# Moving the out projection, the residual sum and its statistics one unit later in a fused Mamba and mixture-of-experts kernel

## The chip, the cores and the metric

The kernel runs on one core of a Trainium2 chip. The metric is the time of one execution on the device, in microseconds (us). The engines are named as in the profile: PE is TensorE, DVE is VectorE, ACT is ScalarE, POOL is GpSimd, SP is the engine that issues most DMAs.

## What is computed

The input x has 2 sequences of 2048 tokens with 128 numbers each. The reference, cut down:

```python
def mamba_layer(x):                       # x: layer norm of the input
    u  = ln(x) * n1_g + n1_b
    xin, z = split(u @ in_proj_w.T)       # 256 channels each
    xc = silu(causal_conv4(xin) + conv_b)
    dt, B, C = split(xc @ x_proj_w.T)     # 8, 16, 16
    delta = softplus(dt @ dt_w.T + dt_b)
    # for each of the 16 states n, along the tokens t:
    #   h[n] = exp(delta * A[n]) * h[n] + delta * B[n] * xc ;  y += h[n] * C[n]
    y = (y + xc * D) * silu(z)
    x = x + y @ out_w.T                   # out projection and residual sum
    n = ln(x) * n2_g + n2_b               # the statistics of this norm move
    gate, val = split(n @ ffg_w.T + ffg_b)
    return x + silu(gate) * val @ ffp_w.T + ffp_b

x = x + mamba_layer(layernorm(x))
x = x + top2_of_8_experts(layernorm(x))   # width 344, routed token by token
```

All is in float32.

## The kernel before

The 4096 tokens are cut into 8 chunks of 512, four sub-blocks of 128. A chunk has 16 **units**, one for each state, numbered here 0 to 15 (so that the fourth unit is unit 3). A unit i does this for both halves of the 256 channels:

- GpSimd multiplies `du` with a row of B that a DMA has spread over the partitions: `inflow` (L818), 128x1024. It is written two units ahead, into one of three buffers, so it waits for the product of unit i - 3 relative to its own (`times_c`).
- ScalarE writes `decay` (L941) into two PSUM banks, one unit ahead.
- VectorE does the scan over the tokens (L1077), two instructions of 128x512. One operand lies in PSUM, one in SBUF.
- VectorE multiplies the states with a spread row of C: `product` (L1087), with both operands in SBUF. TensorE adds the product up in PSUM (L1284, "total"). In some units two or four of the four sub-blocks take another way: TensorE turns the states (L1313, "h_turn"), ScalarE scales them into `h_rows` (L906), TensorE adds them (L1288). Then the product has only half its width (128x512), or there is none.

A chunk's work ahead of its units (the first norm, the convolution, delta: the "front" of chunk c + 1, table `FRONT`) and behind them (gate, out projection, second norm, feed-forward layer, third norm, routing: the "back" of chunk c - 1, table `BACK`) is dealt out over the units of chunk c, a row of the table for each unit. The tokens of earlier chunks go through the experts meanwhile: `silu_m` (L1213), `h_cols` (L1218), `y_rows` (L997), and the "add" (L848), an indirect DMA that GpSimd issues. Routed tokens are sent by "scatter" (L842), another indirect DMA of GpSimd, from table `SEND` or, for the last chunks, `SEND_HELD`; neither has anything in unit 4.

A row of `BACK` has three parts: ahead of the unit's scan, behind the scan, and at the unit's end. One list `order` holds all steps; each engine walks through it and issues the instructions of its own steps in that order. The steps within unit i, from the function `plan`:

```python
        fetch("inflow", i + 2)
        ...
            put("total0", i - 1)
        ...
        put_all(back[0], front[0])
        add()
        put("scan", i)
        ...
        put_all(back[1])
        ...
        first_half(m)
        put_all(back[2], front[2])
        ...
        send()
        ...
        put("times_c", i)
```

The steps that the change touches:

- `y_cols0`, `y_cols1` (L951, ScalarE): the gated y, turned, from PSUM to SBUF.
- `out_proj` (L1332, TensorE): 16 matmuls of 128x128 into the PSUM bank `work_side`. It waits for both `y_cols`.
- `x_two` (L1099, VectorE): the residual sum, 128x512, from SBUF and `work_side`. It waits for `out_proj`.
- `stats2` (L1007 and L1010, VectorE): four statistics and four aggregates.
- `rstd2` (L801 and L803, GpSimd): the variance plus epsilon, to the power -1/2. It waits for the aggregates.
- `shift2` (L1013, VectorE): minus mean times `rstd`, 128x4, both operands in SBUF. It waits for `rstd2`; behind it come `n_tok` (L957, ScalarE, written into the tile m_tok) and `n_turn` (L1224, TensorE).

The front has its own steps in these units: `in1a` and `in1b` (L1248, TensorE) at the ends of units 2 and 3, `conv1` and `tanh_c` (L883, L886, ScalarE) in unit 4, and `xc` (L1045, VectorE) behind shift2 in unit 5. The back of the last chunk, `BACK_LAST`, runs behind the units.

Of the kernel before, what the change touches and what calls it, by code (L numbers as in the profile page):

```python
# [32 lines left out]
def sure_tiles(c):  # L33
# [52 lines left out]
BACK = [  # L86
    ((), ("y_gate",), ("y_turn0",)),
    ((), ("y_cols0",), ("y_turn1",)),
    ((), ("y_cols1",), ("out_proj",)),
    ((), ("x_two", "stats2"), ()),  # L90
    (("rstd2",), (), ()),
    ((), ("shift2",), ("n_tok",)),
    (("n_turn",), ("n_t",), ("ff_gate",)),
    (("x_sum",), ("gate_h",), ("ff_val",)),
# [7 lines left out]
    ((), ("count", "place"), ()),  # L102
]
BACK_LAST = [
    *BACK[:3],
    ((), ("x_two", "stats2", "rstd2"), ()),
    *BACK[5:9],
    ((), ("x_four", "stats3", "rstd3"), ()),
# [1352 lines left out]
```

How the kernel before makes its waits and increments, by code:

```python
        def list_steps(e, step_no, key):  # L548
            if step_no == "0":
                at = LIST_OPS * (key - ROUNDS[0])
                k = SPAN_OF[key]
                taken = base[:, 1, k, :] if key == max(ROUNDS[0], SPANS[k][0]) else tiles_done
                e.wait_ge(S["count"], 2 * (key + 1))
                if at:
                    e.wait_ge(S["list"], at)
                else:
                    e.wait_ge(S["bases"], BASES)
                e.tensor_scalar(tiles_f[:], count[:], 1.0 / P, -ROUND_UP, ALU.mult, ALU.add).then_inc(S["list"], 1)
                if key == CHUNKS - 2:
                    e.tensor_scalar(old_end, count[:], 1.0 / P, ROUND_UP, ALU.mult, ALU.add).then_inc(S["ends"], 1)
                    e.wait_ge(S["ends"], 1)
                    e.tensor_scalar(old_end, old_end, WHOLE, -WHOLE, ALU.add, ALU.add).then_inc(S["ends"], 1)
                e.wait_ge(S["list"], at + 1)
                e.tensor_scalar(tiles_f[:], tiles_f[:], WHOLE, -WHOLE, ALU.add, ALU.add).then_inc(S["list"], 1)
                e.wait_ge(S["list"], at + 2)
                e.tensor_tensor(left[:, 0, 4:], tiles_f[:], taken, ALU.subtract).then_inc(S["list"], 1)
                for k in range(3):
                    e.wait_ge(S["list"], at + 3 + k)
# [39 lines left out]
        def last_list(e, step_no, key):  # L609
# [2 lines left out]
            n = TILES[key]  # L612
            if step_no == "0":
                e.wait_ge(S["count"], 2 * (key + 1))
                e.wait_ge(S["list"], at)
```

## Time and profile before

| | |
|---|---|
| median of 3 runs | 851.82 us (850.19 to 853.87) |
| profiled execution | 846.1 us |
| its span | 844.3 us, 12617 instructions |
| busy share of the span | PE 77%, DVE 88%, ACT 60%, POOL 69% |
| mean granted TensorE clock | 0.889 of full speed |

The span is that of the recorded instructions; the profiled execution's own time has about 1.8 us around it. Busy time counts from an instruction's start to its end as recorded, and so holds any time in which it had started and could not go on. Times in the trace are in us from the start of the span.

### The profile page before, as it was taken

How to read it: one execution, taken by the hardware profiler on the slowest of the kernel's cores; microseconds unless marked ns; L12 is line 12 of the kernel's file. 1: busy time of each engine (PE TensorE's matmuls, PEld its weight loads, DVE VectorE, ACT ScalarE, POOL GpSimd, SP SyncE). 2: the span in 40 equal slices, each digit the busy share in tenths (PEclk: the TensorE clock that was granted, in tenths of full speed). 3: DMA queues.
4: the chain of work that ended last, by engine and by line, in shares of the span. 5: the costliest groups of instructions: out<-in, count | busy, mean ns of one | idle time of the engine just before them, and what ended most of it. 6: DMA issues, size and time to landing. Idle time of an engine off the chain costs nothing.

```text
span 844.3 us, 12617 instructions
## 1 busy us (share of the span) xinstructions
PE 649.8 (77%) x3545; PEld 465.3 (55%) x3545; DVE 739.2 (88%) x1145; ACT 506.5 (60%) x1091; POOL 581.2 (69%) x487
## 2 busy tenths in 40 slices
PE   4438688878778877887877876886876789888991
PEld 2124445545355536764566635873554457788990
DVE  1376998989999999999999999999999897686774
ACT  2545795876688577464846577555854775444440
POOL 1094675677977797689958896789846994456451
PEclk9659899989989898997989988897887899999995
DMA  6923233223323336542464336532424621123247
GB/s 175 263 104 103 87 113 113 82 84 97 116 69 107 106 102 182 158 145 99 130 174 140 109 96 203 148 110 94 133 91 128 171 61 33 39 65 83 65 129 231
DMA packets 80248, 99.94 MB, mean 118 GB/s; under 512 B 10215, under 2 KB 48051, under 8 KB 80163
## 3 DMA queue, kind: packets, MB, share of 16 engines
q1 hardware_dynamic: 75859, 90.21, 36.3%
q0 software_dynamic: 4320, 8.92, 3.0%
q8 instruction: 30, 0.49, 0.2%
q14 instruction: 39, 0.32, 0.1%
HBM read 87.56 MB, written 15.35 MB: 122 GB/s over the span
## 4 chain that ended last, share of the span: by engine, by line
DVE 37%; PE 34%; issue 17%; ACT 7%; DMA 2%; POOL 2%; DVEq 1%; SPq 0%; ACTq 0%; POOLq 0%
DVE state L1077 18%; PE work_front L1248 4%; PE y L1288 4%; DVE product L1087 4%; PE up L1399 2%; PE work_front L1254 2%; PE y L1284 2%; PE up L1410 2%; PE gate L1392 2%; DVE stats L1007 2%; ACT decay L941 1%; DVE silu_m L1213 1%; PE gate L1313 1%; DVE arena L1052 1%; PE work_side L1332 1%
## 5 line engine op out<-in xcount | busy, mean ns | idle before, releaser
L818 POOL TENSOR_TENSOR inflow<-du,b_wide 128x1024 f32<-128x1024 f32 x128 | 315.5, 2468 | 145.0 <-DVE product L1087 92.0
L1077 DVE TENSOR_TENSOR_SCAN state<-decay,carry,inflow 128x512 f32<-128x512 f32 x192 | 234.7, 1264 | 6.5 <-ACT decay L941 6.5
L1087 DVE TENSOR_TENSOR product<-state,c_wide 128x1024 f32<-128x1024 f32 (+1 forms) x93 | 139.1, 1495 | 4.4 <-PE y L1284 3.3
L941 ACT ACTIVATE decay<-arena,a_neg 128x512 f32<-128x512 f32 x128 | 86.6, 688 | 60.7 <-DVE state L1077 56.9
L1284 PE MATMUL y<-ident,product 128*128 128x128 f32 x664 | 106.4, 305 | 20.6 <-DVE product L1087 20.5
L1284 PEld LDWEIGHTS y<-ident,product 128*128 128x128 f32 x664 | 87.2, 158 | 62.5 <-issue 34.7
L848 POOL DMA_INDIRECT y_dram<-y_rows,x_rows x71 | 82.5, 1162 | 56.0 <-ACT y_rows L997 49.1
L941 ACT ACTIVATE decay<-delta_odd,a_neg 128x512 f32<-128x512 f32 x128 | 86.6, 689 | 56.3 <-DVE state L1077 56.1
L1288 PE MATMUL y<-h_rows,ident 128*128 128x512 f32 x180 | 100.9, 652 | 7.0 <-ACT h_rows L906 6.5
L842 POOL DMA_INDIRECT row_dram<-m_tok,place x64 | 74.4, 1163 | 24.3 <-issue 12.7
L1077 DVE TENSOR_TENSOR_SCAN state<-decay,inflow 128x512 f32<-128x512 f32 x64 | 74.5, 1203 | 6.1 <-ACT decay L941 3.6
L1248 PE MATMUL work_front<-u_t,arena 128*128 128x512 f32 x128 | 67.9, 659 | 6.0 <-ACT u_t L876 4.4
L906 ACT ACTIVATE h_rows<-up,c_tok 128x256 f32<-128x256 f32 x110 | 45.9, 469 | 17.7 <-PE up L1313 17.6
L1313 PEld LDWEIGHTS up<-ident,state 128*128 128x128 f32 x220 | 29.9, 156 | 30.9 <-issue 16.8
L1392 PE MATMUL gate<-x_cols,w_stage 128*128 128x128 f32 x246 | 37.3, 291 | 10.5 <-ACT x_cols L987 10.5
L1410 PE MATMUL up<-w_down,h_cols 128*128 (+1 forms) x246 | 38.2, 294 | 9.2 <-DVE h_cols L1218 8.8
L1313 PE MATMUL gate<-ident,state 128*128 128x128 f32 x140 | 24.8, 306 | 23.7 <-DVE state L1077 23.7
L1313 PE MATMUL up<-ident,state 128*128 128x128 f32 x220 | 38.1, 302 | 6.3 <-DVE state L1077 6.3
L1288 PEld LDWEIGHTS y<-h_rows,ident 128*128 128x128 f32 x180 | 31.2, 208 | 18.3 <-ACT h_rows L906 16.4
L1392 PEld LDWEIGHTS gate<-x_cols,w_stage 128*128 128x128 f32 x246 | 33.1, 204 | 13.8 <-ACT x_cols L987 13.7
L1248 PEld LDWEIGHTS work_front<-u_t,arena 128*128 128x128 f32 x128 | 24.5, 212 | 28.2 <-issue 19.0
L1410 PEld LDWEIGHTS up<-w_down,h_cols 128*128 128x128 f32 (+1 forms) x246 | 32.8, 202 | 13.1 <-issue 13.1
(232 smaller groups left out, 1342.6 us busy)
## 6 DMA issues: line engine op xcount, KB each, us to landing
b_wide<-bc_dram SPq DMA_DIRECT2D x128, 256.0 KB, 3.3
c_wide<-bc_dram SPq DMA_DIRECT2D x93, 256.0 KB, 3.5
w_stage<-gate_up_dram SPq DMA_DIRECT2D x26, 344.0 KB, 4.2
x_rows<-row_dram SPq DMA_DIRECT2D x71, 65.0 KB, 1.9
arena<-gate_up_dram SPq DMA_DIRECT2D x8, 344.0 KB, 4.4
x_tok<-in_x SPq DMA_DIRECT2D x8, 256.0 KB, 5.8
out<-x_tok SPq DMA_DIRECT2D x8, 256.0 KB, 4.8
inflow<-y_dram SPq DMA_DIRECT2D x6, 256.0 KB, 4.4
```

The costliest lines, as they stand in the source:

```text
L818: e.tensor_tensor(inflow[:, key % 3], du[:, c % 2], b_wide[:, key % ROW_SLOTS:key % ROW_SLOTS + 1, :].to_broadcast([P, HALVES, CHUNK]), AL ...
L842: e.indirect_dma_start(row_dram, bass.IndirectOffsetOnAxis(place[:, c, q, s:s + 1], 0), m_tok[:, c % M_SLOTS, s, :], None).then_inc(S[f"d_ ...
L848: e.indirect_dma_start(y_dram, bass.IndirectOffsetOnAxis(x_rows[:, key % X_SLOTS, ID_AT:ROW].bitcast(u32), 0), y_rows[:, key % Y_SLOTS, :] ...
L941: e.activation(decay_bank[h][:], delta[c % 2][:, h, :], ACT.Exp, scale=a_neg[:, h, n:n + 1]).then_inc(S["decay"], 1)
L1077: e.tensor_tensor_scan(state[:, key % STATE_SLOTS, h, :], decay_bank[h][:], inflow[:, key % 3, h, :], 0.0 if c % (SEQ // CHUNK) == 0 else ...
L1087: e.tensor_tensor(product[:, key % 2, :, :wide], state[:, key % STATE_SLOTS, :, :wide], c_wide[:, key % ROW_SLOTS:key % ROW_SLOTS + 1, :wi ...
L1248: t = e.matmul(front[:], w_tap[:, k, h * P:(h + 1) * P], u_t[:, key % 2, k:k + CHUNK], start=k == 0, stop=k == D_CONV - 1)
L1284: t = e.matmul(y_bank[r][:, y_at(s, h)], product[:, key % 2, h, s * P:(s + 1) * P], ident[:], is_transpose=True, start=n == 0 and s % 2 + ...
L1288: t = e.matmul(y_bank[r][:], ident[:], h_rows[:, 2 * r:2 * r + 2, :].rearrange("p s d -> p (s d)"), start=False, stop=n == D_STATE - 1, sk ...
L1313: t = e.transpose(h_bank[r][:, y_at(s, h)], state[:, key % STATE_SLOTS, h, s * P:(s + 1) * P], ident[:])
L1392: t = e.matmul(gate[:, q * P:(q + 1) * P], w_stage[:, key % W_SLOTS, 0, q * P:(q + 1) * P], x_cols[:, key % 2, :], start=True, stop=True)
L1410: t = e.matmul(up[:, FF_WIDE:], h_cols[:n, key % 2, q, :], w_down[:n, bass.ds(experts[j % PICKS], 1), q, :].rearrange("p o d -> p (o d)"), ...
```

## The change

Three rows of `BACK` change. The out projection moves from the end of unit 2 to the end of unit 3, `x_two` and `stats2` from unit 3 to unit 4, and `rstd2` from the head of unit 4 (ahead of the add on GpSimd) to its end (behind the add). `BACK_LAST` is written so that it stays as it was.

```diff
 BACK = [
     ((), ("y_gate",), ("y_turn0",)),
     ((), ("y_cols0",), ("y_turn1",)),
-    ((), ("y_cols1",), ("out_proj",)),
-    ((), ("x_two", "stats2"), ()),
-    (("rstd2",), (), ()),
+    ((), ("y_cols1",), ()),
+    ((), (), ("out_proj",)),
+    ((), ("x_two", "stats2"), ("rstd2",)),
     ((), ("shift2",), ("n_tok",)),
     (("n_turn",), ("n_t",), ("ff_gate",)),
 ...
 BACK_LAST = [
-    *BACK[:3],
+    *BACK[:2],
+    ((), ("y_cols1",), ("out_proj",)),
     ((), ("x_two", "stats2", "rstd2"), ()),
     *BACK[5:9],
```

## Rows read from the trace of the kernel before

**Rows 1.** The page: busy times by engine, and VectorE's slices.

```profile
PE 649.8 (77%) x3545; PEld 465.3 (55%) x3545; DVE 739.2 (88%) x1145; ACT 506.5 (60%) x1091; POOL 581.2 (69%) x487
...
DVE  1376998989999999999999999999999897686774
```

**Rows 2.** Waits of VectorE: us in total, times, longest.

```profile
DVE x_two L1099 <- PE work_side L1332: 3.4, 3, 1.5
```

**Rows 3.** Timeline, chunk 5, units 2 to 6: start, duration, engine, line, tiles.

```profile
468.29 3.56 DVE L1087 TENSOR_TENSOR product<-state,c_wide 128x1024 f32<-128x1024 f32 x1
...
470.92 1.81 POOL L848 DMA_INDIRECT y_dram<-y_rows,x_rows  x1 [0.17 <-issue]
...
474.42 2.36 POOL L818 TENSOR_TENSOR inflow<-du,b_wide 128x1024 f32<-128x1024 f32 x1
...
475.17 0.68 DVE L1099 TENSOR_TENSOR x_two<-x_one,work_side 128x512 f32<-128x512 f32 x1
...
476.94 1.08 POOL L848 DMA_INDIRECT y_dram<-y_rows,x_rows  x1 [0.16 <-issue]
477.09 1.20 DVE L1087 TENSOR_TENSOR product<-state,c_wide 128x1024 f32<-128x1024 f32 x1
...
480.68 3.10 DVE L1087 TENSOR_TENSOR product<-state,c_wide 128x512 f32<-128x512 f32 x1
480.88 2.35 POOL L818 TENSOR_TENSOR inflow<-du,b_wide 128x1024 f32<-128x1024 f32 x1
...
485.21 1.10 POOL L848 DMA_INDIRECT y_dram<-y_rows,x_rows  x1 [0.20 <-issue]
486.08 2.64 DVE L1013 SCALAR_TENSOR_TENSOR shift<-mean_var,rstd 128x4 f32<-128x4 f32 x1
486.34 2.35 POOL L818 TENSOR_TENSOR inflow<-du,b_wide 128x1024 f32<-128x1024 f32 x1
...
489.78 0.68 DVE L1087 TENSOR_TENSOR product<-state,c_wide 128x512 f32<-128x512 f32 x1
```

**Rows 4.** Groups of instructions: busy us, mean ns of one, idle before.

```profile
L803 POOL TENSOR_TENSOR rstd<-rstd,minus_half 128x4 f32<-128x4 f32 x8 | 8.4, 1047 | 0.7
L1007 DVE BATCH_NORM_STATS2 stats<-x_two 128x6 f32<-128x128 f32 x32 | 7.0, 281 | 0.3
L1099 DVE TENSOR_TENSOR x_two<-x_one,work_side 128x512 f32<-128x512 f32 x8 | 5.4, 676 | 3.4 <-PE work_side L1332 3.4
L801 POOL TENSOR_SCALAR rstd<-mean_var 128x4 f32<-128x4 f32 x8 | 4.7, 583 | 0.4
...
L785 POOL TENSOR_SCALAR rstd<-mean_var 128x4 f32<-128x4 f32 x8 | 1.8, 229 | 6.2 <-DVE mean_var L1010 6.1
...
L1010 DVE BATCH_NORM_AGGREGATE mean_var<-stats 128x2 f32<-128x6 f32 x96 | 9.1, 157 | 0.8
...
L1332 PE MATMUL work_side<-w_out,y_cols 128*128 128x128 f32 x128 | 17.5, 295 | 1.1 <-ACT y_cols L951 1.1
```

**Rows 5.** Timeline, chunk 3, unit 3: a scatter of GpSimd.

```profile
291.61 2.05 POOL L842 DMA_INDIRECT row_dram<-m_tok,place  x1 [0.28 <-POOL m_tok L836]
```

**Rows 6.** Timeline, chunk 1: x_two.

```profile
135.34 0.69 DVE L1099 TENSOR_TENSOR x_two<-x_one,work_side 128x512 f32<-128x512 f32 x1 [1.49 <-PE work_side L1332]
```

**Rows 7.** Busy time by stretch, chunk 7: the column behind POOL is TensorE's granted clock.

```profile
653.00:655.00 2.00, 2.00 (x12) 2.00 (x11) 1.16 (x2) 0.97 (x3) 1.83 (x2) 0.50 0.55 203
```

**Rows 8.** Timeline, chunk 7, units 2 to 7.

```profile
650.57 3.78 PE L1332 MATMUL work_side<-w_out,y_cols 128*128 128x128 f32 x16 [0.74 <-ACT y_cols L951]
...
654.39 0.69 DVE L1099 TENSOR_TENSOR x_two<-x_one,work_side 128x512 f32<-128x512 f32 x1 [0.84 <-PE work_side L1332]
...
654.99 1.06 PE L1313 MATMUL gate<-ident,state 128*128 128x128 f32 x4
...
658.77 1.23 DVE L1087 TENSOR_TENSOR product<-state,c_wide 128x1024 f32<-128x1024 f32 x1
...
667.63 2.46 DVE L1077 TENSOR_TENSOR_SCAN state<-decay,carry,inflow 128x512 f32<-128x512 f32 x2 [2.73 <-ACT decay L941]
```

## The prediction

> **What bounds the kernel now.** I read the page's busy times first: VectorE is busy for 88% of the span, and its line of slices stands at 8 or 9 from slice 5 to slice 33 [rows 1]. So in the eight chunks VectorE is hardly idle by the record, and there a microsecond is won only if VectorE does less or is held up less. The table of waits shows how little it idles for the steps that move: x_two waited three times for the out projection, 3.4 us in all [rows 2]. The timeline then shows what a busy VectorE hides. The same product of half width (128x512) has a row of 0.68 us and one of 3.10 us, and the long one ends when GpSimd's inflow ends [rows 3]. The shift, four numbers a partition, has a row of 2.64 us, and it too ends with an inflow [rows 3]. So the two engines exclude each other when a VectorE instruction reads two tensors in SBUF (product, shift) and GpSimd is at work; scans, x_two (one operand in PSUM) and the statistics run beside an inflow without loss [rows 3]. What the schedule is worth is therefore which instruction of VectorE meets which of GpSimd, and that I follow in units 2 to 5 of one chunk.
>
> **The change part by part.** Nothing is added or removed: 16 matmuls, x_two (0.68 us), 4 statistics (0.28 each), 4 aggregates (0.16 each) and two GpSimd instructions (0.58 and 1.05) move [rows 4]; from x_two's start to the product's is 1.92 us of VectorE [rows 3]. Seven chunks (1 to 7) carry such a block; the last block, behind the loop, keeps its order.
>
> *Chunk 5, unit 3.* Today inflow(5) runs 474.42 to 476.78; VectorE is free for the moved work at 475.17, does x_two and statistics, and reaches its product at 477.09, past the inflow: no hold-up, 1.20 us [rows 3]. After the change the product stands at 475.17 and must wait for 476.78, so it ends at 477.9 and not 478.2: taking 1.92 us out of the unit gives 0.3. The other 1.6 turn into a hold-up. On GpSimd the next in line is the add (an indirect DMA's issue). Today it starts at 476.94, ahead of the product, and takes 1.08. In unit 2 one sees it where a held-up product goes first: 470.92, 1.81 us [rows 3]. After the change unit 3 looks like unit 2, so the add costs 0.73 more, and everything behind it on GpSimd (tag copy, two scatters, inflow(6)) comes 0.7 later: inflow(6) from 480.88 to 481.6, its end at 484.0.
>
> A rule of the Trainium skill bears on this step. The rows: the product of unit 2 ends at 471.85 (468.29 and 3.56), the add held up by it at 472.73 [rows 3], 0.88 us later. The Trainium skill's page SBUF — State Buffer (SBUF: two separate sides) says that the shared port pair is an exclusive lock held for the whole instruction, and that a GpSimd DMA issue locked out by VectorE stays blocked until about 115 ns after VectorE's end. Read as the end of the issue, that figure would put the add's end at 478.0 as today, chunks 4 to 6 would cost nothing, and the sum below would be 1.9 us less; the row (0.88) speaks against this reading, and for the lock.
>
> *Chunk 5, unit 4.* Scan(4) now ends near 480.35; x_two and statistics take it to 482.3, beside inflow(6), unhindered. That is cover: today the product stood there from 480.68 and lost 2.4 us (3.10 less 0.68) [rows 3]. But inflow(6) ends at 484.0, and the product ends at 484.5, against 483.78 today: +0.7. rstd2 now stands behind that add and no longer ahead of it. The order swap is worth nothing by itself, since today add and rstd2 both come before inflow(7) too; nothing is queued by SEND in unit 4, so no scatter waits for rstd2. Sum: add until 485.4 (0.9 after the product, as above), rstd2 0.25 (not held up; its like for the first norm, L785, takes 0.23) [rows 4] and 1.05 with gaps until about 486.95, and inflow(7) at 487.0 against 486.34.
>
> *Unit 5.* Shift2 needs rstd2. Today rstd2 is done before the add at 485.21, and the shift is held up anyway from 486.08 till inflow(7) ends [rows 3]. After the change rstd2's end, the scan's end and inflow(7)'s start fall within 0.1 us of each other; I take it that inflow(7), which needs no signal from another engine, gets in first. The shift ends 0.65 later than today. Bounds: if the shift gets in first, up to 2.4 us are gained in that chunk; if the inflow does, +0.7. I take the second, since today's row shows a shift already waiting and passed by an inflow. Chunks 4 and 6 have the same pattern (an add in unit 3 that starts level with the product), so 3 x 0.65 = +1.9.
>
> *Chunks 2 and 3* have no add in unit 3; there the first scatter behind the product is held up already (291.61, 2.05 us, in chunk 3) [rows 5], and GpSimd's chain keeps its times: inflow(6) starts where it does, and everything behind. 0, bounds -0.3 and +0.3 each.
>
> *Chunk 1.* x_two waits 1.49 us for TensorE [rows 6]. That wait does not vanish whole, because the out projection also comes a unit later, behind in1a and a total. I take -0.3, bounds -1.5 and 0.
>
> *Chunk 7* has no product in unit 3 (all four sub-blocks go over TensorE) and TensorE is slow: granted clock 0.50, the 1.2 GHz level, in 653 to 655 [rows 7]. Today the out projection goes first (650.57, 3.78 us) and x_two follows at 654.39 [rows 8]. After the change TensorE first does unit 3's totals and transposes, which wait for scan(3) (about 653.5). Groups of four take up to 1.06 us there [rows 8]; four overlapping groups make 2.7 us, until 656.2. Then the out projection: 3.78 us at the low clock, 1.95 at the high one (half; the mean matmul of this line, over both clocks, takes 0.295 [rows 4]). It ends between 658.2 and 660.0, while VectorE has been free since scan(4)'s end at 656.0. With 1.92 for x_two and statistics and 1.2 for the product, that product ends at 661.3 to 663.1; today at 660.0 [rows 8]. So +1.3 to +3.1, and I take 2.2. rstd2 and inflow(7) then push the shift back by up to 1.3 more, but scan(7) waits 2.73 us for ScalarE's decay today [rows 8], which hides that.
>
> **Sum:** -0.3 + 0 + 0 + 1.9 + 2.2 = +3.8 us, between -3 (x_two's waits gone, nothing else) and +8 in my bounds. The profiled execution took 846.1 us (844.3 span), which becomes 849.9. It lies under the fastest of the three timed runs, whose median is 851.82, so the median to expect is 851.8 + 3.8 = 855.6.
>
> **The rivals.**
> *Cover wins (faster).* GpSimd's chain is not late, so moved statistics swallow the hold-up of unit 4's product. In chunks 3 to 6 each 2.4 us goes and 1.6 comes in unit 3: 4 x -0.8 = -3.2; with x_two's 3.4 us [rows 2] -6.6, thus 845.2. For it: x_two and statistics run freely beside an inflow. Against it: GpSimd starts inflow(6) the moment it has finished the scatters, so it is the later of the two; the rival decides only if the add of unit 3 stays at 1.1 us and TensorE is in time in chunk 7.
> *Nothing measurable.* The add of unit 3 is over when the product is, about 478.0, because part of its work runs beside the product; chunks 4 to 6 cost nothing and chunk 7 its low end: -0.3 + 1.3 = +1, thus 852.8. For it: the add and the product of unit 3 do run side by side today (1.08 and 1.20 us from 476.94 and 477.09); against it: the add of unit 2 doesn't, 1.81 [rows 3].
> *The front is late (much slower).* On TensorE the out projection now stands ahead of in1b, so conv1, tanh_c and xc come up to 1.95 us later, 3.78 at the low clock. Today the held-up shift covers that: if the cover is short by 1 us in seven chunks, +7 on top, 862.6. Against it: in chunk 5 the shift ends at 488.7, and inflow(7) delays it further.
> *The change does not do what it says* can't be: the three lists fix the order of every queue.
>
> **How the numbers follow.** Chances: the forecast (+2 to +6) 0.48, cover wins 0.18, nothing measurable (-2 to +2) 0.21, front late 0.13. I call 0.5% (4.3 us) what a measurement of this kernel tells from no change. Of the forecast half lies beyond +4.3: slower 0.24 + 0.13 = 0.37. Faster 0.17, the rival nearly whole. Same 0.46. The range leaves out the outer parts of the first and last case: 846.5 to 861.
>
> **What would show it.** Right: product in unit 3 of chunks 4 to 6 grows from 1.2 to about 2.75 us; the add behind it from 1.08 to 1.8; the half product in unit 4 of chunk 5 falls from 3.10 to 2.2 or 2.3; L1099's waits vanish in chunks 2 to 6 and rise to 2 us or more in chunk 7; shift still held up 2.4 us. Wrong: a shift of 0.15 to 0.3 us in unit 5 (it got in first), an add of 1.1 in unit 3, or xc waiting for ScalarE.

## The result, and the profile after

Over 16 runs of each, the kernel after took a median of 856.87 us (853.9 to 860.28) and the kernel before 851.91 us (850.19 to 854.34). The ratio is 1.0056, with a 95% interval of 1.0041 to 1.007: about 4.8 us slower (3.5 to 6.0), and 1.3 us above the 855.6 us forecast. The ratio lies just over the 0.5% that the prediction set as its bound, and that bound is inside the interval.

The profiled execution of the kernel after took 856.39 us (span 854.6). Against the one before (846.1) that is 10.3 us, twice what the medians say, so the two traces can't be subtracted end from end. Most of the excess lies where both kernels have the same instructions in the same order: from the end of the last chunk's scans to the end of the span it took 142.5 us before and 148.6 after, and between 140.6 and 150.0 in the eight variants below, whose code there is the same as well. So I compare the traces inside the chunks only, by the start of scans.

The page of the kernel after:

```profile
PE 654.9 (77%) x3545; PEld 472.7 (55%) x3545; DVE 740.2 (87%) x1145; ACT 505.4 (59%) x1091; POOL 582.7 (68%) x487
...
DVE  1377999999999999999999999989998997676764
```

VectorE is as busy as in [rows 1] and has the same count of instructions. The table of VectorE's waits, after (its lines are one higher than those before):

```profile
DVE xc L1046 <- ACT arena L887: 16.0, 2, 13.5
...
DVE x_two L1100 <- PE work_side L1333: 6.1, 3, 3.6
...
DVE x_two L1100 <- issue: 0.3, 1, 0.3
```

The waits for the out projection did not go: 6.1 us and a longest of 3.6, against 3.4 and 1.5 in [rows 2]. One of the three waits in each trace belongs to the last block, behind the chunks, where nothing moved (1.1 us before, 1.9 after). The table below says where time was lost. It has the distance from the start of unit 0's scan to that of unit 9's in each chunk, for the kernel before, and what the kernel after adds to it.

| chunk | before: unit 0, unit 9 | after: unit 0, unit 9 | added |
|---|---|---|---|
| 1 | 118.74, 159.40 | 118.40, 158.20 | -0.9 |
| 2 | 195.94, 238.50 | 193.35, 235.94 | 0.0 |
| 3 | 273.32, 317.20 | 271.68, 315.57 | 0.0 |
| 4 | 360.24, 410.64 | 358.55, 409.54 | +0.6 |
| 5 | 454.55, 504.38 | 453.45, 503.81 | +0.5 |
| 6 | 547.41, 597.26 | 547.86, 597.77 | +0.1 |
| 7 | 638.42, 676.86 | 638.91, 681.05 | +3.7 |

Timeline of chunk 5, units 3 to 5, after; it answers to [rows 3]:

```profile
473.33 2.35 POOL L819 TENSOR_TENSOR inflow<-du,b_wide 128x1024 f32<-128x1024 f32 x1
...
474.08 2.69 DVE L1088 TENSOR_TENSOR product<-state,c_wide 128x1024 f32<-128x1024 f32 x1
...
475.84 1.87 POOL L849 DMA_INDIRECT y_dram<-y_rows,x_rows  x1 [0.16 <-ACT y_rows L998]
...
479.05 0.66 DVE L1100 TENSOR_TENSOR x_two<-x_one,work_side 128x512 f32<-128x512 f32 x1
...
480.47 2.35 POOL L819 TENSOR_TENSOR inflow<-du,b_wide 128x1024 f32<-128x1024 f32 x1
...
480.95 2.43 DVE L1088 TENSOR_TENSOR product<-state,c_wide 128x512 f32<-128x512 f32 x1
...
484.64 1.04 POOL L804 TENSOR_TENSOR rstd<-rstd,minus_half 128x4 f32<-128x4 f32 x1
...
485.68 2.34 POOL L819 TENSOR_TENSOR inflow<-du,b_wide 128x1024 f32<-128x1024 f32 x1
485.72 2.32 DVE L1014 SCALAR_TENSOR_TENSOR shift<-mean_var,rstd 128x4 f32<-128x4 f32 x1
...
489.10 0.68 DVE L1088 TENSOR_TENSOR product<-state,c_wide 128x512 f32<-128x512 f32 x1
```

Read it against [rows 3]. The product of unit 3 has grown from 1.20 to 2.69 us: it starts 0.75 us into the inflow and ends 1.1 us behind the inflow's end. The add behind it has grown from 1.08 to 1.87. Then GpSimd is late: inflow(5) ran 1.09 us earlier than before (473.33 against 474.42), inflow(6) only 0.41 earlier (480.47 against 480.88): 0.7 us lost between them, and the add alone took 0.8 longer. In unit 4 the half product fell from 3.10 to 2.43 us, and it starts 0.27 us later, so it ends 0.4 us earlier, again 0.7 less than the 1.1 of the start. At the end of the stretch the product of unit 5 starts 0.68 us earlier than in [rows 3]: of the 1.1 us lead 0.4 to 0.5 is gone.

Timeline of chunk 7, units 3 to 7, after; it answers to [rows 8]:

```profile
654.09 1.11 PE L1314 MATMUL gate<-ident,state 128*128 128x128 f32 x4 [1.25 <-DVE state L1078]
...
656.71 3.27 PE L1333 MATMUL work_side<-w_out,y_cols 128*128 128x128 f32 x16
...
660.01 0.69 DVE L1100 TENSOR_TENSOR x_two<-x_one,work_side 128x512 f32<-128x512 f32 x1 [3.62 <-PE work_side L1333]
...
661.93 1.19 DVE L1088 TENSOR_TENSOR product<-state,c_wide 128x1024 f32<-128x1024 f32 x1
...
663.30 1.05 POOL L804 TENSOR_TENSOR rstd<-rstd,minus_half 128x4 f32<-128x4 f32 x1
664.34 2.35 POOL L819 TENSOR_TENSOR inflow<-du,b_wide 128x1024 f32<-128x1024 f32 x1
...
665.41 1.30 DVE L1014 SCALAR_TENSOR_TENSOR shift<-mean_var,rstd 128x4 f32<-128x4 f32 x1
...
670.83 2.46 DVE L1078 TENSOR_TENSOR_SCAN state<-decay,carry,inflow 128x512 f32<-128x512 f32 x2 [1.74 <-ACT decay L942]
...
671.83 2.38 POOL L819 TENSOR_TENSOR inflow<-du,b_wide 128x1024 f32<-128x1024 f32 x1
...
673.32 3.20 DVE L1088 TENSOR_TENSOR product<-state,c_wide 128x1024 f32<-128x1024 f32 x1
```

The out projection starts only at 656.71, behind the transposes of unit 3, and VectorE stands idle for 3.62 us ahead of `x_two`. TensorE's granted clock meanwhile (the column behind POOL's busy time; 0.50 is the 1.2 GHz level):

```profile
656.00:658.00 2.00, 2.00 (x12) 2.00 (x11) 0.39 (x1) 1.13 (x4) 1.98 (x2) 0.50 0.49 168
658.00:660.00 2.00, 2.00 (x12) 2.00 (x12) 0.00 (x0) 1.10 (x3) 0.51 (x1) 0.63 0.54 192
```

The inflow of 664.34 and the last two rows of the timeline have these counterparts before, in units 5 and 7:

```profile
660.17 2.34 POOL L818 TENSOR_TENSOR inflow<-du,b_wide 128x1024 f32<-128x1024 f32 x1 [0.80 <-DVE product L1087]
...
667.64 2.36 POOL L818 TENSOR_TENSOR inflow<-du,b_wide 128x1024 f32<-128x1024 f32 x1
...
670.12 2.20 DVE L1087 TENSOR_TENSOR product<-state,c_wide 128x1024 f32<-128x1024 f32 x1
```

The whole chunk began 0.5 us later than before (638.91 and 638.42), so 0.5 us is to be taken off each difference of times here. Scan(7) is 3.2 us later than in [rows 8] (670.83 and 667.63), but the last inflow shown is 4.2 us later (671.83 and 667.64). Before, it was over at 670.00, ahead of the product; now it runs until 674.21, and the product takes 3.20 us in place of 2.20. From there on chunk 7 is 4.2 us less 0.5 (where it began) late.

### The profile page after: what moved, and what is told of

It reads as the page before. It is cut to its first block, busy times and chain, and to the rows that moved or that the text cites. A ratio compares the mean times of both kernels' runs of the same rounds, so it can differ in the third digit from the quotient of the medians.

```text
span 854.6 us, 12617 instructions
## 1 busy us (share of the span) xinstructions
PE 654.9 (77%) x3545; PEld 472.7 (55%) x3545; DVE 740.2 (87%) x1145; ACT 505.4 (59%) x1091; POOL 582.7 (68%) x487
## 4 chain that ended last, share of the span: by engine, by line
PE 37%; DVE 32%; issue 15%; ACT 8%; POOL 4%; DMA 1%; SPq 1%; DVEq 1%; another core or an unknown queue 0%; ACTq 0%; POOLq 0%
DVE state L1078 15%; PE work_front L1249 5%; DVE product L1088 4%; PE y L1289 4%; PE y L1285 3%; PE gate L1393 2%; PE up L1411 2%; PE up L1400 2%; ACT decay L942 2%; PE work_front L1255 2%; DVE stats L1008 2%; POOL inflow L819 2%; PE y L1393 1%; PE gate L1314 1%; PE y L1400 1%
## 5 line engine op out<-in xcount | busy, mean ns | idle before, releaser
L849 POOL DMA_INDIRECT y_dram<-y_rows,x_rows x71 | 84.7, 1193 | 62.4 <-ACT y_rows L998 56.5
L1289 PE MATMUL y<-h_rows,ident 128*128 128x512 f32 x180 | 97.3, 632 | 3.9 <-ACT h_rows L907 3.2
L843 POOL DMA_INDIRECT row_dram<-m_tok,place x64 | 72.6, 1135 | 24.3 <-issue 13.1
L1393 PE MATMUL gate<-x_cols,w_stage 128*128 128x128 f32 x246 | 39.1, 300 | 12.1 <-ACT x_cols L988 11.8
L1400 PE MATMUL up<-x_cols,w_stage 128*128 128x128 f32 x246 | 38.3, 296 | 2.2 <-ACT y_rows L998 1.4
```

The lines of the kernel that those rows point to most:

```text
L843: e.indirect_dma_start(row_dram, bass.IndirectOffsetOnAxis(place[:, c, q, s:s + 1], 0), m_tok[:, c % M_SLOTS, s, :], None).then_inc(S[f"d_ ...
L849: e.indirect_dma_start(y_dram, bass.IndirectOffsetOnAxis(x_rows[:, key % X_SLOTS, ID_AT:ROW].bitcast(u32), 0), y_rows[:, key % Y_SLOTS, :] ...
L1289: t = e.matmul(y_bank[r][:], ident[:], h_rows[:, 2 * r:2 * r + 2, :].rearrange("p s d -> p (s d)"), start=False, stop=n == D_STATE - 1, sk ...
L1393: t = e.matmul(gate[:, q * P:(q + 1) * P], w_stage[:, key % W_SLOTS, 0, q * P:(q + 1) * P], x_cols[:, key % 2, :], start=True, stop=True)
```

## The experiments

Eight variants ran. The first four shared a chip with 35 runs of the kernel before (median 851.5 us), the last four another chip with 35 more (median 844.78 us). The chips differ, so only ratios and traces are compared. The ratio is not exactly the quotient of the two medians; where the text below says what a variant gained or lost in all, it is the ratio times the median of before. "Chunks" is what each adds between the scans of units 0 and 9, worked out as in the table above.

| variant | median us | ratio (95%) | chunk 1 | 4 | 5 | 6 | 7 |
|---|---|---|---|---|---|---|---|
| new rows in chunk 7 only | 856.2 | 1.0039 (1.002 to 1.0057) | -2.3 | 0.0 | 0.0 | -0.2 | +3.7 |
| in chunks 4 to 6 only | 851.95 | 1.0013 (0.9992 to 1.0034) | -2.3 | +0.7 | +0.6 | +0.1 | 0.0 |
| in chunks 1 to 3 only | 851.61 | 0.9992 (0.9973 to 1.0011) | -2.3 | +0.4 | 0.0 | +0.2 | +0.1 |
| out projection stays in unit 2 | 852.64 | 1.0012 (0.9993 to 1.0031) | -2.3 | +0.7 | +0.6 | +0.6 | +0.2 |
| projection ahead of the transposes | 846.85 | 1.002 (0.9994 to 1.0045) | -0.8 | +0.6 | +0.6 | 0.0 | +0.2 |
| no add in unit 3 of chunks 4 to 6 | 848.7 | 1.0041 (1.0018 to 1.0065) | -2.3 | +0.6 | +0.8 | +0.2 | +3.5 |
| root ahead of the add | 849.49 | 1.006 (1.0041 to 1.008) | -2.3 | +0.8 | +0.7 | +0.7 | +2.7 |
| mixed rows | 846.11 | 1.0012 (0.999 to 1.0034) | -2.3 | 0.0 | 0.0 | -0.2 | +0.2 |

Chunks 2 and 3 lie between 0.0 and +0.1 in all of them. The table also shows how far one execution can be read: chunk 4 of the third variant has the old rows, and +0.4.

**The new rows in chunk 7 only.**

```diff
+BACK_OLD = [
+    *BACK[:2],
+    ((), ("y_cols1",), ("out_proj",)),
+    ((), ("x_two", "stats2"), ()),
+    (("rstd2",), (), ()),
+    *BACK[5:],
+]
+MOVED = (6,)
...
-        backs.extend([[(name, c) for name in part] for part in row] for row in (BACK if c < CHUNKS - 1 else BACK_LAST))
+        backs.extend([[(name, c) for name in part] for part in row] for row in ((BACK if c in MOVED else BACK_OLD) if c < CHUNKS - 1 else BACK_LAST))
```

> The new rows are used only for the block that lies in chunk 7 (the back of chunk 6); chunks 1 to 6 keep the old rows. In the traces of before and after, the scans of chunk 7 go from +0.5 us (unit 3) to +4.2 us (unit 9), with x_two waiting 3.6 us for TensorE. My theory (the out projection stands behind unit 3's transposes on TensorE, partly at the 1.2 GHz level): +2.5 to +4 us over before, x_two waits about 3 us. Rival, that the loss lies in chunks 4 to 6 or behind the loop: within 1 us of before.

The ratio is 1.0039, +3.3 us (1.7 to 4.9), which leaves no room for the rival's 1 us, and the trace shows the same wait in the same place:

```profile
658.24 3.33 PE L1341 MATMUL work_side<-w_out,y_cols 128*128 128x128 f32 x16
...
661.60 0.69 DVE L1108 TENSOR_TENSOR x_two<-x_one,work_side 128x512 f32<-128x512 f32 x1 [3.69 <-PE work_side L1341]
```

By the ratios one block of the seven carries two thirds of the whole loss (3.3 of 4.8 us; the intervals leave this share wide).

**In chunks 4 to 6 only**, with the same lists.

```diff
-MOVED = (6,)
+MOVED = (3, 4, 5)
```

> The new rows only for the blocks in chunks 4, 5 and 6, where experts' adds run. My theory (the add of unit 3 is held up by the product, 1.08 to 1.8 us, and pushes inflow(6), rstd2 and inflow(7) back): +1.9 us over before, 0.5 to 0.7 in each of the three chunks by the scans. Rival, cover wins: -2 us or less. Rival, all of the loss is chunk 7's: within 0.5 us of before.

By the ratio it is 1.1 us above before, and the interval (-0.7 to +2.9) holds both nothing and the 1.9 us forecast; it excludes "cover wins". So the time alone does not show this loss. The scans do: +0.7, +0.6 and +0.1 where the rows are new, 0.0 in chunk 7. The trace has the predicted sequence again (chunk 5, unit 3 and 4):

```profile
475.01 2.70 DVE L1096 TENSOR_TENSOR product<-state,c_wide 128x1024 f32<-128x1024 f32 x1
...
476.77 1.88 POOL L857 DMA_INDIRECT y_dram<-y_rows,x_rows  x1 [0.15 <-ACT y_rows L1006]
...
481.89 2.44 DVE L1096 TENSOR_TENSOR product<-state,c_wide 128x512 f32<-128x512 f32 x1
```

**In chunks 1 to 3 only.**

```diff
-MOVED = (6,)
+MOVED = (0, 1, 2)
```

> The new rows only for the blocks in chunks 1, 2 and 3, which have no adds. My theory: x_two's waits for TensorE get shorter there, -0.3 to -1.5 us in all over before. Rival, that the wins of chunks 1 and 2 in the traces (-2.3 and +1.0 by the scans) are differences between two executions and not of the change: 0. Rival, the front is late behind the out projection: +1 us or more and xc waiting for ScalarE.

The interval, 0.9973 to 1.0011, allows a gain of 2.3 us and a loss of 0.9. It is inconclusive about the -0.3 of chunk 1, and leaves just no room for a late front of +1. What the traces say of it: seven of the eight variants have -2.3 in chunk 1, and two of these, the first and the second, keep the old rows there. In these two `x_two` of chunk 1 does not wait at all. The wait of 1.49 us in [rows 6] belongs to the one execution that was profiled before, not to the order.

**The out projection stays in unit 2**; the residual sum, its statistics and the root move.

```diff
-    ((), ("y_cols1",), ()),
-    ((), (), ("out_proj",)),
+    ((), ("y_cols1",), ("out_proj",)),
+    ((), (), ()),
     ((), ("x_two", "stats2"), ("rstd2",)),
```

> The out projection stays at the end of unit 2; residual sum and statistics go to unit 4 and rstd2 behind them as in the change. My theory: chunk 7's wait of x_two for TensorE vanishes (3.6 us) while chunks 4 to 6 still cost 0.6 us each, so -0.5 to +2 us over before, and about 3 to 4 us under the change. Rival, that the place of the statistics or of rstd2 makes the loss in chunk 7: as slow as the change, +4 to +5 us.

Chunk 7's loss is gone (+0.2) and chunks 4 to 6 keep theirs (+0.7, +0.6, +0.6); by the ratio it is 1.0 us above before (-0.6 to +2.6), so the rival's +4 to +5 is out. So the moved projection costs chunk 7, the moved statistics cost chunks 4 to 6.

**The projection moves, but in chunk 7 goes ahead of unit 3's transposes.** The row of unit 3 has it in its middle part there, and at the end as in the change in all other chunks.

```diff
+BACK_TURN_LATE = [
+    *BACK[:3],
+    ((), ("out_proj",), ()),
+    *BACK[4:],
+]
...
-        backs.extend([[(name, c) for name in part] for part in row] for row in (BACK if c < CHUNKS - 1 else BACK_LAST))
+        backs.extend([[(name, c) for name in part] for part in row] for row in (BACK_LAST if c == CHUNKS - 1 else BACK_TURN_LATE if c == CHUNKS - 2 else BACK))
```

> The change, but in chunk 7 the out projection stands in unit 3 ahead of that unit's turns of the state on TensorE, not behind them. My theory: only TensorE's order makes chunk 7's loss, so x_two waits under 1 us there, the scans of chunk 7 end within 0.5 us of where they begin (the change: +3.7), and the kernel is +0.5 to +2 us over before. Rival, that one unit's delay of statistics and rstd2 is enough in chunk 7 (shift2 late behind inflow(7)): +2 us or more by the scans of chunk 7, +4 to +5 us in all.

Chunk 7 adds 0.2 in place of 3.7. In the trace the projection is even slower than in the change, yet nobody waits:

```profile
652.05 3.56 PE L1338 MATMUL work_side<-w_out,y_cols 128*128 128x128 f32 x16
...
655.73 0.66 DVE L1105 TENSOR_TENSOR x_two<-x_one,work_side 128x512 f32<-128x512 f32 x1
...
661.35 1.28 DVE L1019 SCALAR_TENSOR_TENSOR shift<-mean_var,rstd 128x4 f32<-128x4 f32 x1
```

It starts 13.7 us behind the scan of unit 0 in place of 17.8 (652.05 less 638.34, 656.71 less 638.91). The time in all, +1.7 us (-0.5 to +3.8), leaves the rival's +4 to +5 out. So chunk 7's loss is one of TensorE's order, and a low clock alone doesn't make it. The shift is held up here too (1.28 us), and it costs nothing that the scans show.

**No add in unit 3 of chunks 4 to 6.** The add of each of these units is put off; it comes later in the same chunk. The computation is whole.

```diff
-        add()
+        if not (c in (4, 5, 6) and n == 3):
+            add()
```

> The change, but in unit 3 of chunks 4 to 6 GpSimd issues no add; each is put off to the next unit. Nothing else is put off. My theory: the held-up issue behind product(3) is what makes inflow(6) late; without it inflow(6) of chunk 5 starts about 0.9 us earlier than in the change and ends about as product(4) gets ready, so that product(4) takes under 1.6 us instead of 2.4 and scan(5) is 0.1 to 1 us earlier than before's instead of 0.7 later. Over the whole kernel the added issues in later units may give it back: 0 to -2 us against the change. Rival, that the loss of 0.7 in unit 4 comes from the statistics standing ahead of the product on VectorE: scan(5) stays 0.7 later.

In chunk 5, units 3 to 6:

```profile
473.30 2.69 DVE L1089 TENSOR_TENSOR product<-state,c_wide 128x1024 f32<-128x1024 f32 x1
...
474.85 1.19 POOL L838 COPY m_tok<-tag 128x8 uint32<-128x8 uint32 x1
...
478.70 2.36 POOL L820 TENSOR_TENSOR inflow<-du,b_wide 128x1024 f32<-128x1024 f32 x1
...
480.18 1.44 DVE L1089 TENSOR_TENSOR product<-state,c_wide 128x512 f32<-128x512 f32 x1
...
483.96 2.32 DVE L1015 SCALAR_TENSOR_TENSOR shift<-mean_var,rstd 128x4 f32<-128x4 f32 x1
...
486.44 1.96 POOL L850 DMA_INDIRECT y_dram<-y_rows,x_rows  x1 [0.18 <-issue]
...
490.42 3.44 DVE L1089 TENSOR_TENSOR product<-state,c_wide 128x512 f32<-128x512 f32 x1
```

Here the cover does win. Without the add, inflow(6) starts at 478.70, and the half product behind the moved statistics takes 1.44 us in place of 2.43 (0.68 when free). Scan(5) of chunk 5 starts at 481.54, 11.63 us behind scan(3); it is 11.94 before (471.77 to 483.71) and 12.62 in the change (470.68 to 483.30). So without the add in unit 3 the move gains 0.3 us there, and with it loses 0.7. But the add has to go somewhere: it comes in unit 5 (486.44, 1.96 us), what follows it on GpSimd is late, the product of unit 6 meets the next inflow and takes 3.44 us in all, and at unit 9 the chunk is 0.8 us late after all. The ratio makes +3.5 us (1.5 to 5.5), against about +4.8 for the change; the intervals overlap, and the scans of chunks 4 to 6 (+0.6, +0.8, +0.2) show no gain over the change.

**The root ahead of the add.**

```diff
-    ((), ("x_two", "stats2"), ("rstd2",)),
+    (("rstd2",), ("x_two", "stats2"), ()),
```

The two sets of steps lie on different engines, so `rstd2` ahead of the add in the list means GpSimd computes it first and waits for the statistics, which VectorE makes in the same unit.

> The change, but rstd2 stands at the head of unit 4 on GpSimd, ahead of the add, as in before. My theory: that place is worth nothing, since the shift is held up by inflow(7) either way; scans of chunks 4 to 6 within 0.2 us of the change, the kernel within 1 us of it. Rival, that rstd2 behind the add makes the shift late: 0.5 us less in each of chunks 4 to 6, some -1.5 us against the change.

```profile
485.30 1.04 POOL L804 TENSOR_TENSOR rstd<-rstd,minus_half 128x4 f32<-128x4 f32 x1
...
486.55 1.10 POOL L849 DMA_INDIRECT y_dram<-y_rows,x_rows  x1 [0.20 <-issue]
487.41 2.64 DVE L1014 SCALAR_TENSOR_TENSOR shift<-mean_var,rstd 128x4 f32<-128x4 f32 x1
...
487.68 2.35 POOL L819 TENSOR_TENSOR inflow<-du,b_wide 128x1024 f32<-128x1024 f32 x1
```

The root is over at 486.34, the shift starts when VectorE comes free at 487.41, and the inflow holds it up for 2.64 us as in [rows 3]. The ratio, 1.006, is within the interval of the change, and the forecast gain of the rival (-1.5 us) did not come; chunks 4 to 6 show +0.8, +0.7 and +0.7, for chunks 4 and 5 0.2 more than the change. So the old place of the root is no better, and by the scans 0.2 us worse.

This variant shows one thing more. In chunk 7, where there is no add, it has the order of the change, but its projection met a faster TensorE:

```profile
658.20 2.25 PE L1333 MATMUL work_side<-w_out,y_cols 128*128 128x128 f32 x16
```

It started at the same 17.8 us behind unit 0's scan and took 2.25 us in place of 3.27 (the granted clock is 0.79 in 658 to 660 and 1.00 in 660 to 662), `x_two` waited 2.6 us and not 3.6 for it, and chunk 7 adds 2.7 us, 1.0 less.

**Mixed rows:** the projection stays in unit 2 everywhere, the statistics move in chunks 1, 2, 3 and 7, and chunks 4 to 6 keep the old rows. `BACK` is that of the fourth variant here, `BACK_OLD` that of the first.

```diff
...
-        backs.extend([[(name, c) for name in part] for part in row] for row in (BACK if c < CHUNKS - 1 else BACK_LAST))
+        backs.extend([[(name, c) for name in part] for part in row] for row in (BACK_LAST if c == CHUNKS - 1 else BACK_OLD if c in (3, 4, 5) else BACK))
```

> The out projection stays at the end of unit 2 everywhere. Statistics and rstd2 go to unit 4 for the blocks in chunks 1, 2, 3 and 7 and stay in unit 3 in chunks 4 to 6. It takes the runs' best part for each chunk. My theory: without chunk 7's wait and without the three held-up adds only chunk 1's win is left: -2 to 0 us against before, which five rounds can hardly tell from nothing. Rival, that the wins by the scans in chunks 1 and 2 are of TensorE's clock in one execution: 0.

By the ratio it is 1.0 us above before, the interval 0.999 to 1.0034: no gain. It keeps clear of both losses, and nothing comes in for it, since where the moved statistics cost nothing they save nothing either (chunk 7 +0.2).

## Why the prediction was right, step by step

**Chunk 5, unit 3: right.** Taking 1.92 us of work out of the unit gained 0.4 us at the scan behind it (scan(4) starts at 476.69, some 1.5 us ahead of before, and scan(3) was 1.1 ahead already) where 0.3 was forecast. The product took 2.69 us (forecast: about 2.75), the add 1.87 (1.8). Chunks 4 and 6 have adds of 1.88 and 1.87 us in this place; the product grew to 2.81 in chunk 4, but only to 1.85 in chunk 6.

**The lock: right.** The add ends 0.94 us after the product (476.77 and 477.71), as far behind as in [rows 3] (0.88); free adds take 1.08 there. So nearly all of the issue's own time lies behind VectorE's end; whether it starts over then or had not got beyond its start, no row tells. By the Trainium skill's page SBUF — State Buffer (SBUF: two separate sides), the port pair is held for the whole instruction, and for a product that began first the trace agrees (it began 1.76 us ahead of the add, and the add ended behind it). It does not for an issue that began first: the product that follows the add by 0.15 us in [rows 3] is not held up, 1.20 us. The page's 115 ns, read as the end of a locked-out issue, would have left the add at 1.1 us, and no row here shows that.

**Unit 4: right.** The half product took 2.43 us for 2.2 to 2.3 forecast, and ended late by GpSimd's 0.7, counted from unit 0's scan. The sixth variant is the test of this step: with GpSimd on time the product takes 1.44 and the sign turns. It shows too that "cover wins" was no empty rival. It needed an add of unit 3 that isn't slowed, as its condition said.

**Unit 5: right.** Inflow(7) got in 0.04 us ahead of the shift (485.68 and 485.72) and held it up 2.32 us. It came 0.4 us later than before (485.68 less 453.45, 486.34 less 454.55) where 0.66 was forecast, since from the end of unit 4's product to it 2.3 us passed and not 2.5. In the sixth and seventh variants the shift is held up as well (2.32 and 2.64 us); the gain of up to 2.4 us did not come in any of the three.

**Chunks 4 to 6: the mechanism right, the sum of 1.9 a little high.** Measured: 0.6, 0.5 and 0.1 in the change. Chunk 6 reads differently by execution: in some the distance from scan(2) to scan(3) is 1.3 us shorter than in the trace before, in some it isn't. Where it is, kernels with the new rows there add 0.0 to +0.2 and those with the old rows -0.2; where it isn't, +0.6 or +0.7 and +0.2. Before itself, with the old rows, is of the second kind (0.0). So the rows cost 0.2 to 0.7 there, and the three chunks 1.3 to 1.8 in all. Why the distance differs is not known. The variant with these chunks alone measured +1.1, between -0.7 and +2.9.

**Chunks 2 and 3: right**, 0.0 each.

**Chunk 1: the -0.3 isn't borne out.** The change shows -0.9, but the two other executions with the old rows show -2.3 there. Of the seven with the new projection, the new statistics or both, two stand at -0.8 or -0.9 and five at -2.3. By that neither a gain nor a cost of the new rows is shown. The step that failed is to take a wait of one execution [rows 6] for a wait of the order.

**Chunk 7: the term that was mis-sized**, 2.2 forecast with bounds of 1.3 and 3.1, and 3.7 measured. It has two parts, both counted from unit 0's scan.

The first part is VectorE's. The projection started as worked out (656.71 less 638.91 is 17.80; 656.2 less 638.42 is 17.78) and ended within its bounds; it ran at the low clock for most of its 3.27 us. So the product of unit 4 ended 2.6 us late (663.12 less 638.91, against 660.00 less 638.42), where 2.2 was taken: 0.4 of the miss lies in the choice within the bounds.

The second part, the missing 1.1 us, is the step that failed: "rstd2 and inflow(7) then push the shift back by up to 1.3 more, but scan(7) waits 2.73 us for ScalarE's decay today [rows 8], which hides that." The push came, and for scan(7) the wait did hide it: the wait shrank to 1.74 us, and scan(7) came 2.7 us late, no more than VectorE's own part. It didn't hide it on GpSimd. Before, inflow(7) starts 0.17 us behind the end of unit 4's product (660.17 and 660.00). After, the second instruction of the root stands between them, 1.05 us long, and it is 1.22 us (664.34 and 663.12). That puts the inflows behind it 2.6 and 1.1, so 3.7 us late. One of them, the last in the timeline above, met the product of unit 7 and made it 3.20 us long, and the 1.1 us that the wait had hidden was back. The seventh variant has the same 1.22 us and 1.0 less of the first part. The fifth has them too; there the product of unit 4 ends 0.9 us ahead of before, since the statistics have left unit 3, and 0.2 us is left. A chain on two engines needs cover on both.

**The sum.** The total came nearer than its terms, and that is in part luck: chunks 4 to 6 were put some 0.4 us too high and chunk 7 1.5 too low. With 1.5 for chunks 4 to 6 and 3.7 for chunk 7 it is 5.2 us, and 4.8 was measured. The 3.4 us of [rows 2], in the lower bound of -3 and in the rival's 6.6, hold the 1.1 us of the last block, which the change does not touch; the signs of being right also had waits of `x_two` vanish in chunks 2 to 6, where the trace before has none. By itself chunk 7 measured +3.3 (first variant), chunks 4 to 6 +1.1. Of the rivals, the late front can be struck out: `xc` waited for ScalarE twice, 16.0 us in all and 13.5 at the longest, and before twice as well, 15.1 and 12.6; the shorter of the two waits is 2.5 us in both, and both stand ahead of chunk 1, the first with a moved block. "Nothing measurable" fails on the add of unit 3 (1.87, not 1.1) and on chunk 7.

**Still open:** what chunk 1 costs, and whether the granted clock in chunk 7 depends on the order. With the old place there the projection took 3.78 us in four executions, [rows 8] among them, and 2.05 us in the third variant's. Behind the transposes it took 3.11 to 3.33 us in three and 2.25 in the seventh variant's. With the old place the faster projection was worth nothing at unit 9 (third variant: +0.1); behind the transposes it was worth 1.0 us (+2.7 and not +3.7). So the price of the change in chunk 7 varies with the clock, and these few executions don't say how often each case comes. No variant holds the clock fixed.

## What to carry to other kernels

Work that is moved out of one stall may uncover another: before a VectorE instruction with two operands in SBUF is brought forward, look which GpSimd instruction it will now run into, and which one will queue behind it. When a step of TensorE is moved, look in each chunk for what else the new place holds: in chunks 2 to 6 nothing waited more than 0.3 us for the moved projection, and the one of chunk 7, behind transposes that wait for a scan, brought two thirds of the loss. A slack on one engine hides a delay only if every engine in the loop has that slack.

## What the runs showed of the hardware

An indirect DMA issue of GpSimd and a product of VectorE that begin within 0.15 us of each other, the issue first, run side by side (1.08 and 1.20 us) [rows 3]. The same issue begun 0.9 us before the end of a product that is on its way ends 0.94 us behind it (1.87 us, chunk 5 after). Across the traces of before, the change and the sixth variant, an issue that began while a product was running ended 0.83 to 0.95 us behind that product, whether it had begun 0.2 us ahead of the product's end or 1.2 us; with no product beside it an issue takes 0.95 us or more. A GpSimd copy of 128x8 numbers, 0.18 us when free, took 1.19 us in the place of the add, behind the same product, and ended with it. And the shift, four numbers a partition, took 0.12 to 0.16 us where no inflow ran and 2.32 us behind an inflow that had begun 0.04 us earlier. A recorded start is no claim on the place: in [rows 3] the shift starts 0.26 us ahead of the inflow and still ends with it.

The same instructions at the same place need not see the same clock: the out projection of chunk 7 in its old place took 3.78 us in four profiled executions and 2.05 in a fifth. And the part behind the scans, with the same code in all ten profiled executions, took from 140.6 to 150.0 us, a spread of about twice the effect studied here; one profile of each kernel could not have found it without a comparison stage by stage.
